# Cross attention over 32 context tiles: start-up loads, key and value evictions, query packing and decay sums placed anew

## The reference, cut to what matters

```python
q = x @ Wq.T                                  # x is layer-normalised first
k_raw, v_raw = context @ Wk.T, context @ Wv.T # 32 heads of 8, interleaved halves
q, k = rmsnorm(q), rmsnorm(k)                 # per head, over the 8 columns
attn = softmax(einsum('bhnd,bhmd->bhnm', q, k) * 8 ** -0.5)
x = x + einsum('bhnm,bhmd->bhnd', attn, v)
```

## Time and profile before

| what | value |
| --- | --- |
| median of 3 runs | 423.85 us (423.51 to 424.43) |
| the profiled execution | 424.59 us |
| its span in the trace | 422.8 us |
| cross attention in it | about 0 to 182 us |
| steady length of a step of the loop | about 4.7 us |

### The profile page before, as it was taken

One profiled execution on the slowest core, in us unless ns is written; L12 is line 12 of the kernel. 1 busy time (PEld: TensorE's weight loads), 2 busy tenths in 40 slices (PEclk: granted clock), 3 DMA queues, 4 the chain that ended last, 5 costly groups with the idle time before them and its releaser, 6 DMA issues.

```text
span 422.8 us, 14336 instructions
## 1 busy us (share of the span) xinstructions
PE 392.6 (93%) x6016; PEld 328.7 (78%) x6016; DVE 301.0 (71%) x685; ACT 264.3 (63%) x543; POOL 206.6 (49%) x257
## 2 busy tenths in 40 slices
PE   7979999999999999888999988799889998999997
PEld 4657667777667777668999987678778887989995
DVE  6687989997888887756988887586996757212220
ACT  2467878878888888965546533532999236444441
POOL 2377757666567765105554610610498636445530
PEclk9989999999999999999999999999999999999999
DMA  4097651542321100370000044030000490000000
...
DMA packets 10832, 34.78 MB, mean 82 GB/s; under 512 B 2192, under 2 KB 7312, under 8 KB 8976
## 3 DMA queue, kind: packets, MB, share of 16 engines
...
HBM read 33.60 MB, written 0.26 MB: 80 GB/s over the span
## 4 chain that ended last, share of the span: by engine, by line
PE 69%; DVE 15%; POOL 7%; issue 4%; ACT 3%; DMA 1%; SPq 0%; DVEq 0%; POOLq 0%; ACTq 0%
PE ps L1669 9%; PE ps L1624 8%; PE ps L1147 8%; PE ps L1133 6%; PE ps L406 5%; PE ps L1656 3%; PE ps L1639 3%; PE ps L392 3%; PE ps L467 3%; PE ps L875 3%; PE ps L857 2%; PE ps L352 2%; PE ps L816 2%; PE ps L823 2%; PE ps L435 1%
## 5 line engine op out<-in xcount | busy, mean ns | idle before, releaser
L1590 ACT ACTIVATE sb_arena<-ps 128x1024 f32<-128x1024 f32 x128 | 123.5, 1019 | 22.1 <-PE ps L1656 21.9
L1669 PE MATMUL ps<-sb_arena 128*25 128x128 f32 (+1 forms) x2048 | 69.6, 276 | 0.9 <-issue 0.8
L1669 PEld LDWEIGHTS ps<-sb_arena 128*25 128x25 f32 (+1 forms) x2048 | 50.7, 98 | 8.5 <-issue 1.4
L1624 PE MATMUL ps<-sb_halves 128*128 128x512 f32 x192 | 54.6, 420 | 1.7 <-DVE sb_arena L1395 1.0
L1179 POOL TENSOR_TENSOR sb_halves<-sb_big,sb_halves 128x704 fp32r<-128x704 f32 x20 | 33.7, 1687 | 38.7 <-ACT sb_halves L1173 38.7
L1245 DVE SCALAR_TENSOR_TENSOR sb_arena<-ps,sb_w_q,sb_arena 128x176 f32<-128x176 f32 x40 | 15.9, 401 | 42.7 <-ACT sb_arena L1197 42.5
L1624 PEld LDWEIGHTS ps<-sb_halves 128*128 128x128 f32 x192 | 34.6, 193 | 14.6 <-issue 6.2
L1147 PE MATMUL ps<-sb_halves 128*128 128x352 f32 x240 | 42.9, 332 | 2.0 <-POOL sb_halves L1179 2.0
L496 POOL TENSOR_TENSOR sb_halves<-sb_big,sb_halves 128x256 fp32r<-128x256 f32 x28 | 21.0, 771 | 45.5 <-ACT sb_halves L480 45.5
L1484 POOL TENSOR_TENSOR sb_big<-sb_arena 128x256 f32<-128x256 f32 x31 | 19.0, 612 | 49.2 <-DVE sb_arena L1356 49.2
L1147 PEld LDWEIGHTS ps<-sb_halves 128*128 128x128 f32 x240 | 39.1, 189 | 3.3 <-DVE sb_arena L1245 1.7
...
## 6 DMA issues: line engine op xcount, KB each, us to landing
...
```

The lines of the kernel that those rows point to most:

```text
L1590: nc.scalar.activation(probs[:, n % P_SLOTS].rearrange("p a g n -> p a (g n)"), ps[:, bank:bank + 2], ACT.Exp, scale=XD ** -0.5).then_inc( ...
L1624: i = T.matmul(ps[:, 7], ctx_half[:, t % 2, c, kt], wkv_half[:, d, kt], start=(n + kt == 0), stop=(n == 2 and kt == KT - 1))
L1669: i = T.matmul(ps[32 * gg:32 * gg + m, 6, j * P:(j + 1) * P], v_sb[:, t % V_SLOTS, 4 * gg + j, head], probs[:, n % P_SLOTS, a, gg], start= ...
```

## The change

The load of `w_xkv` and `w_xq` goes from ScalarE's queue to SP's, behind `x` and the identity; the tiny `decay` goes to ScalarE's. `x` and the identity get a semaphore each. The decay rate is worked out before the transposed `x` is copied, and the first two scans come ahead of the queries' mean squares. ScalarE instead of VectorE takes the raw keys of tiles 0 and 1 out of the PSUM and squares them from there (`first_keys`), and takes the values of tiles 1 to 4 (`first_values`; VectorE takes those of tile 0). ScalarE also copies batch 1's turned queries and the sums of batch 0 (one copy of 512 columns). Batch 1's queries are packed by GpSimd in five single instructions behind tiles 7 to 11, and turned in step 13 into a bank of scores. The decay weights are summed in 16 pieces of 128, one a step in steps 14 to 29, where the scans have ended.

```diff
+ACT_VALUES = (1, 2, 3, 4)
+TURN_AT = 13
...
-        gsums = sb("gsums", [P, 4])
+        gsums = sb("gsums", [P, MB])
...
             sp.dma_start(x[:], io["x"].rearrange("b l d -> l b d")).then_inc(sem("x_loaded"), 16)
-            sp.dma_start(id32[:], io["id32"]).then_inc(sem("x_loaded"), 16)
+            sp.dma_start(id32[:], io["id32"]).then_inc(sem("id32_loaded"), 16)
+            sp.dma_start(w_xkv, io["w_xkv"]).then_inc(sem("wkv_loaded"), 16)
+            sp.dma_start(w_xq, io["w_xq"]).then_inc(sem("wq_loaded"), 16)
             sp.dma_start(ctxT[:, 0], io["ctx"][0]).then_inc(sem("ctx_loaded0"), 16)
-            sp.dma_start(decay[:], io["decay"]).then_inc(sem("decay_loaded"), 16)
             sp.dma_start(ctxT[:, 1], io["ctx"][1]).then_inc(sem("ctx_loaded1"), 16)
...
-            sp.wait_ge(sem("geo_summed"), 4)
+            sp.wait_ge(sem("geo_summed"), MB)
...
-            dve.wait_ge(sem("x_loaded"), 32)
+            dve.wait_ge(sem("x_loaded"), 16)
             layer_norm(dve, LN_OF["xattn"])
-            ln_copy(dve, 0, 0)
...
+            def sum_weights(n):
+                V.tensor_reduce(gsums[:, n:n + 1], geo[:, n * P:(n + 1) * P], AX_X, ALU.add).then_inc(sem("geo_summed"), 1)
...
-            def take_q(b):
-                dve.wait_ge(sem("q_transposed"), b + 1)
-                V.tensor_copy(qT_x[:, b], ps[:, 7].bitcast(F16).rearrange("p (g n) -> p g n", g=GROUPS)
-                              ).then_inc(sem("q_ready"), 1)
...
+            decay_rate()
+            ln_copy(dve, 0, 0)
             dve.wait_ge(sem("wkv_high"), 1)
             V.tensor_tensor(wkv_half[:, 1], w_xkv, wkv_half[:, 0].bitcast(F32), ALU.subtract).then_inc(sem("wkv_split"), 1)
-            decay_rate()
+            decay_weights(0)
+            decay_weights(1)
             mean_squares_q(0)
-            decay_weights(0)
-            take_k(0)
             norm_q(0)
             mean_squares(0)
+            dve.wait_ge(sem("k_taken"), 1)
+            take_v(0)
             pack_q(0)
             pack_keys(0)
-            take_k(1)
+            mean_squares(1)
             take_keys(0)
-            take_v(1)
-            mean_squares(1)
-            decay_weights(1)
             pack_keys(1)
             for t in range(NB):
                 if t + 2 < NB:
                     take_k(t + 2)
-                    take_v(t + 2)
+                    if t + 2 not in ACT_VALUES:
+                        take_v(t + 2)
                     if t + 2 < MB:
                         decay_weights(t + 2)
+                    else:
+                        sum_weights(t + 2 - MB)
                     mean_squares(t + 2)
-                if t == 6:
-                    take_q(1)
                 if t + 1 < NB:
                     take_keys(t + 1)
-                if t == MB:
-                    take_acc(0)
                 if t + 2 < NB:
                     pack_keys(t + 2)
-                if t == 1:
+                if t == 4:
                     mean_squares_q(1)
-                if MB <= t < MB + 4:
-                    n = t - MB
-                    V.tensor_reduce(gsums[:, n:n + 1], geo[:, n * 512:(n + 1) * 512], AX_X, ALU.add
-                                    ).then_inc(sem("geo_summed"), 1)
...
             split_context(1)
+            weigh_context(0)
             split_context(2)
-            square_keys(1)
+            weigh_context(1)
             split_context(3)
-            weigh_context(0)
-            weigh_context(1)
             for t in range(2, NB):
...
-                if t == 4:
-                    pack_q1()
+                if t == TURN_AT - 6:
+                    norm_q1()
+                if TURN_AT - 5 <= t < TURN_AT - 3:
+                    high_q1(t - TURN_AT + 5)
+                if TURN_AT - 3 <= t < TURN_AT - 1:
+                    low_q1(t - TURN_AT + 3)
...
-            act.dma_start(w_xkv, io["w_xkv"]).then_inc(sem("wkv_loaded"), 16)
-            act.dma_start(w_xq, io["w_xq"]).then_inc(sem("wq_loaded"), 16)
+            act.dma_start(decay[:], io["decay"]).then_inc(sem("decay_loaded"), 16)
             ln_rstd(act, LN_OF["xattn"])
+            act.wait_ge(sem("decay_loaded"), 16)
+            nc.scalar.activation(dec[:, 0:1], decay[:], ACT.Exp, scale=-1.0).then_inc(sem("decay_exp"), 1)
...
+            def first_keys(t):
+                act.wait_ge(sem("kv_projected"), t + 1)
+                nc.scalar.activation(ksq[:, t], ps[:, 7, 0:256], ACT.Square).then_inc(sem("k_squared"), 1)
+                nc.scalar.copy(kraw[:, t], ps[:, 7, 0:256]).then_inc(sem("k_taken"), 1)
+
+            def first_values(t):
+                if t >= V_SLOTS:
+                    act.wait_ge(sem("pv_done"), SUBS * (t - V_SLOTS + 1))
+                act.wait_ge(sem("k_taken"), t + 1)
+                for r in range(2):
+                    i = nc.scalar.copy(v_sb[:, t % V_SLOTS, :, 25 * r:25 * r + 8],
+                                       ps[:, 7, 256 + 128 * r:384 + 128 * r].rearrange("p (h d) -> p h d", d=XD))
+                i.then_inc(sem("kv_taken"), 1)
+
             take_queries(0)
             q_rstd(0)
-            act.wait_ge(sem("k_taken"), 1)
-            nc.scalar.activation(ksq[:, 0], kraw[:, 0], ACT.Square).then_inc(sem("k_squared"), 1)
...
+            first_keys(0)
...
+            def turned_queries(b, bank):
+                act.wait_ge(sem("q_transposed"), b + 1)
+                nc.scalar.copy(qT_x[:, b], ps[:, bank].bitcast(F16).rearrange("p (g n) -> p g n", g=GROUPS)
+                               ).then_inc(sem("q_ready"), 1)
+
             key_rstd(0)
             take_queries(1)
...
+            first_keys(1)
+            act.wait_ge(sem("v_cleared"), 1)
+            first_values(1)
             key_rstd(1)
+            turned_queries(0, 4)
             for t in range(NB):
                 for c in range(SUBS):
                     exps(SUBS * t + c)
+                    if c == 0 and t + 2 in ACT_VALUES:
+                        first_values(t + 2)
                     if c == 1 and t + 2 < NB:
                         key_rstd(t + 2)
-                    if t == 2 and c == 0:
+                    if t == 6 and c == 0:
                         q_rstd(1)
+                    if t == TURN_AT and c == 2:
+                        turned_queries(1, 2 * ((SUBS * t + 1) % 3))
+                    if t == MB and c == 0:
+                        act.wait_ge(sem("pv_done"), SUBS * MB)
+                        nc.scalar.copy(accs[:, 0], ps[:, 6]).then_inc(sem("acc_taken"), 2)
...
-            pe.wait_ge(sem("x_loaded"), 32)
+            pe.wait_ge(sem("id32_loaded"), 16)
...
-                if t == 6:
-                    pe.wait_ge(sem("q1_packed"), 1)
-                    pe.wait_ge(sem("kv_taken"), t + 3)
-                    turn_queries(1, 7)
...
                 values(SUBS * t)
+                if t == TURN_AT:
+                    pe.wait_ge(sem("q1_packed"), 2)
+                    pe.wait_ge(sem("exp_done"), SUBS * t + 2)
+                    turn_queries(1, 2 * ((SUBS * t + 1) % 3))
                 if t != MB and t + 3 < NB:
                     project(t + 3)
+                if t == TURN_AT:
+                    pe.wait_ge(sem("q_ready"), 2)
```

40 lines of the change are left out of this document (14 added, 26 removed).

## The result

The change makes the kernel faster by a third of what was forecast: 421.59 us (median of 8 runs, 420.97 to 423.19) against 423.83 (8 runs, 423.50 to 424.51), ratio 0.9946, 95% interval 0.9934 to 0.9958. That is 2.2 us where 7.2 were expected, outside the range. The profiled execution took 421.62, its span is 420.0; before it was 422.8, so the traces differ by 2.8 us.

What follows compares the result with a forecast made beforehand. TensorE, busy 93% of the span, was taken as the bound, so gains come from its waits and low clock. Terms -3.5 - 1.9 - 0.5 - 1.3 = -7.2 us gave a median of 416.7, range 413.7 to 420.0.

Steps and rivals of the forecast that it cites:

- Item 1: Loads and layer norm at the start: VectorE waits for x alone, so the layer norm starts 1.8 us earlier.
- these four loads in one queue cost nothing: Start of the kernel: w_xkv, w_xq and tile 0 land no later than what needs them, at no cost.
- Rival D: Start: loads in one queue land one after the other, tile 0 at about 22 us; total 432, chance 0.04.
- Item 2: TensorE's clock at the start: its gap shrinks, so dummies, queries and first projection shorten, 2.1 us taken.
- Rival A: Clock stays low through the first projection, so item 2 gives nothing; 418.8 us, chance 0.15.
- Item 3: First keys and values: scores of step 0 come earlier, term -3.5 us (-1.4 to -4.2).
- item 5: Steps 3 to 13, packing batch 1's queries: GpSimd late for nobody, VectorE slowed 1.8; term -0.5 us (+0.7 to -1.7).
- Item 4: Steps 0 to 2: TensorE's wait for keys falls away and the clock holds; term -1.9 us (0 to -2.6).
- Item 6: Steps 16 to 20: small sums cost nothing, ScalarE's copy costs some 0.4; term -1.3 us (0 to -2.2).
- Nothing behind the loop changes: All behind the loop: no change in time, term 0.
- Rival E: ScalarE's extra work merely takes VectorE's place and only the start counts; 420.3 us, chance 0.06.
- rival B: VectorE slowed more: GpSimd's five instructions cost 3.0, ScalarE's step 16 stall 1.3; 418.8 us, chance 0.1.

Runs made afterwards that it cites:

- the late weighing: Kernel after with GpSimd weighing tiles 0 and 1 behind all four splits: 420.70 us, ratio 0.9920; with batch 1's root also in step 5, 419.71.
- all four: Kernel after with weighing late, batch 1's root in step 5, ScalarE values of tiles 1 and 2 only, VectorE copying batch 0's sums: 418.71 us; again 418.35.
- small loads first: Kernel with all four edits, five small loads of later stages moved to the front of the weight loads: 421.43 us, ratio 0.9940.
- loads done early: Kernel with all four edits, weight loads issued two beside a tile from tile 12 on: 419.88 us; same edit in the kernel after: 424.14.

## Why the prediction was wrong, point by point

**Item 1, the layer norm: right.** It starts at 3.78 (3.93 forecast, less what VectorE saved ahead of it).

**Item 1, "these four loads in one queue cost nothing": the step that failed first.** The working took the GB/s of the kernel before, which came from two queues, and read off it when each load's last byte would have gone if the loads moved strictly one after another: `w_xkv` at 4.7 and tile 0 at 5.8, half a microsecond more to land. They landed at about 6.5 and 7.7, 1.3 and 1.4 us late. Both assumptions were wrong. The rate of one queue was 296 GB/s from 3.0 to 5.6 us, not 378 (putting the weights back in a second queue brings it back, 387). And an amount of bytes does not say when a load is there: 0.85 MB had gone at 5.2 and 1.25 MB at 6.5, some 1.3 and 1.2 us before `w_xkv` and tile 0 could be used, where half a microsecond was allowed; that the loads overlap, so that a load's last bytes go later than its place says, would explain it and is not shown. Of the lateness some 0.5 to 0.7 is thus the rate and the rest the landing. By the forecast the first projection was to end 3.9 us earlier, and it ended 2.33 earlier, 1.6 missing. About 1.0 of this is a collision that late loads brought about: GpSimd's split of tile 0 now lies beside VectorE's split of the weights and takes 2.17 us (7.77 to 9.94) instead of 1.19. Tile 0's place alone was not the cause, since both kernels that moved it forward gained nothing. Rival D had the right place and a far too large size.

**Item 2, the clock: right in its mechanism.** The dummies, the queries and the first projection shortened by 0.56, 0.81 and 1.11. Rival A did not happen. With the two queues of before and thus the gap, the queries and the projection were slow again (2.08, 2.45), the dummies were not (0.84).

**Item 3, scores 0: wrong, -1.14 instead of -3.5.** Of the 2.36 missing, 1.6 is item 1. The other 0.8 is the contention of GpSimd's weighing with VectorE: it costs 1.14 by the experiment, against 0.4 that the sum had allowed for VectorE's new order and that does not show (with the late weighing it takes 6.12 us from the end of the first projection to the scores, before 6.08). That the row reads -1.14 is itself one execution against one, with the spread given below the table. The working had listed what VectorE's new order costs, and never costed GpSimd's, though the diff moves `weigh_context(0)` and `(1)` ahead of the splits of tiles 2 and 3, and though item 5 used the very row that prices it.

**Item 4, steps 0 to 2: right**, -1.67 against -1.9. `turn_keys` waits 0.53 and 0.52 in steps 1 and 2 (0.45 was forecast), VectorE's waits are gone. What the text did not see is that the clock is only likely to hold: ahead of step 0 TensorE is busy 2.04 us of 4, and in one run of eight the mean clock is lower (0.995), in 14 of 36 over the kernels with this start.

**Item 5, steps 3 to 13: the second step that failed,** -0.03 instead of -0.5. "GpSimd is late for nobody" took `t == 7` in GpSimd's list for step 7 of TensorE. GpSimd's index runs two tiles ahead, so it reached the instruction at 49.85, as step 6 began, while ScalarE makes the root behind that step's first exponential, at 51.93: 2.38 us of waiting in GpSimd's queue, 0.9 of it on TensorE's path (step 6). Put right, the stretch is 54.80 (alone) and 54.57 (with the late weighing), 1.1 and 1.3 less than before. The term itself was thus pessimistic, and the missing wait ate it: the root moved from step 2 to step 6 in the diff, and its reader was not looked up.

**Item 6, steps 16 to 20: -1.19 against -1.3, and that is luck.** The sums are free as forecast, but ScalarE's copy costs 0.96, not 0.4. Seven other executions with the same code in these steps took 25.19 to 25.95 us, 0.2 to 0.9 less than before. The difference is idle time of TensorE that no semaphore explains, of which the profiled execution of after had little here (see the stalls at the end of this section).

**"Nothing behind the loop changes": wrong by 1.3.** Steps 21 to 28 are 0.64 longer, the tail 0.62, and the tail's part comes back in every kernel built on after. Its largest single row is an idle of 1.02 us at 173.77 (0.78 at 177.18 before). The rest of it stays open.

**Rival E came nearest** (420.3): the sum of what failed is about that of what it left out, but not by its mechanism, since ScalarE took little and VectorE was in fact relieved. The range's upper end, 420.0, was set by a low clock, which did not come, and by rival B's two costs, of which the copy came in large part (0.96 where B had 1.3); it had no room for a wait that the diff creates unseen.

**The stalls without a releaser.** These are the idle times of TensorE that end the account of item 6. They stand before the same instructions in several kernels, they grow in the two kernels that move loads, and they need no weight load. The page lists, beside the data queue, one of 48 packets of instructions, 0.79 MB, over the same DMA engines:

```profile
q8 instruction: 48, 0.79, 0.7%
```

The traces say what these packets are. Each has 16,384 bytes, and TensorE's records, matmuls, weight loads and all else, number 12,344 in the kernel after, which is 48.2 x 256. Count them up to each stall:

| kernel | TensorE goes on at | idle | instructions before it | packet ends |
| --- | --- | --- | --- | --- |
| before | 177.18 | 0.78 | 8,641 | 175.70 |
| after | 173.77 | 1.02 | 8,641 | 172.36 |
| all four | 120.25 | 0.51 | 5,825 | 118.86 |
| all four | 129.83 | 0.44 | 6,337 | 128.50 |
| all four, again | 107.27 | 0.74 | 5,057 | 105.91 |
| small loads first | 81.86 | 0.73 | 3,521 | 80.34 |
| small loads first | 110.20 | 1.20 | 5,057 | 108.93 |
| loads done early | 71.19 | 1.45 | 3,009 | 69.96 |

Every count is 193 more than a multiple of 256. The eighteen traces list 62 idle times of TensorE marked "issue" between 34 and 185 us, those before `turn_keys` left out. The count is of this form for all 62, and each ends 1.2 to 1.6 us after the end of the packet of the same number. So TensorE stood still for the next 256 instructions of its program. No experiment delays a packet alone, but count and time leave hardly another reading. How late a packet starts decides the stall: ahead of instruction 5,057 it started with 168 instructions still to run in the kernel after (no stall listed), with 68 in the second execution of all four (0.74), with 29 in the kernel with the small loads first (1.20). There 0.68 MB of loads had moved between 106 and 108 us, and the packet started at 107.95, as they ended.

It also prices the edits. At the 27 places from instruction 1,729 to 8,385 (about 48 to 168 us), take the time by which two starts of TensorE's instructions lie further than 0.08 us apart. It sums to 0.32 us before, 1.05 in the kernel after, 2.35 and 3.05 in the two executions of all four edits, 6.10 with the small loads first and 3.62 with the loads done early; in the kernel after with the loads done early it is 3.80. The small loads first cost 2.7 us (against all four edits the sums differ by 3.1 to 3.8), the loads done early in the kernel after 2.5 (2.8). At the other places of the program, taken 256 apart in the same way, the sum averages 0.15.

**Still open.** Why a packet starts late where no weight load is near, as at 120 and 130 us; an experiment that changes only the packets is missing. In two executions of the same kernel the stalls differ (0.51 and 0.44 in one; 0.74, 0.34, 0.20 and 0.43 in the other), so small effects in this stretch can't be read from one trace.
